# A recurrent attention and expert block: new places for the first batch's transposes, the output weights' maximum, two stores, and VectorE's normalisation

## The reference

```python
xn = (x - mean(x)) / sqrt(var(x) + 1e-5)
q, k, v = split(xn @ Wqkv.T + b_qkv)
scores = q k^T / sqrt(32) + alibi_bias, masked to the lower triangle
s = (softmax(scores) @ v) @ Wout.T + b_out
e = argmax(softmax(xn @ w_router.T))            # one expert for each token
h = xn @ w_fc[e].T ;  a = where(h >= 0, h, h/2) ** 2
g = silu(top_weight * (a @ w_proj[e].T))
out = x + s * g
```

## Time and profile before

| | |
|---|---|
| median of 3 runs | 1421.49 us (1421.0 to 1421.74) |
| profiled execution | 1422.13 us, its span 1420.4 us |
| busy: PE, DVE, ACT, POOL | 1364.2 us (96%), 932.4 (66%), 777.3 (55%), 684.0 (48%) |
| attention passes 1 to 6 | 82.65 us each |
| PE waits named in the whole span, the largest | 14.6 us at the first rows, 8.8 us scores on masks, 3.8 us psT L547 on DVE am L892, 3.4 us psA L437 on DVE xn L869 |

### The profile page before, as it was taken

One profiled execution on the slowest core, in us unless ns is written; L12 is line 12 of the kernel. 1 busy time (PEld: TensorE's weight loads), 2 busy tenths in 40 slices (PEclk: granted clock), 3 DMA queues, 4 the chain that ended last, 5 costly groups with the idle time before them and its releaser, 6 DMA issues.

```text
span 1420.4 us, 30128 instructions
## 1 busy us (share of the span) xinstructions
PE 1364.2 (96%) x9775; PEld 872.8 (61%) x9775; DVE 932.4 (66%) x2456; ACT 777.3 (55%) x1835; POOL 684.0 (48%) x894
## 2 busy tenths in 40 slices
PE   4879999999999999999799999999999999999997
PEld 3446556655655665565466666666666666666665
DVE  6768777777777777777778755555445555544444
ACT  4678878787887878787756422323323223232222
POOL 1455666566566656656633444443334433334333
PEclk9989999999999999999999999999999999999999
DMA  4525334343533434354266322221121121112110
GB/s 179 166 60 173 111 120 147 107 142 98 179 105 120 149 105 142 98 149 130 99 225 212 109 58 55 57 61 33 43 57 54 51 59 53 39 44 56 49 34 30
DMA packets 119458, 140.56 MB, mean 99 GB/s; under 512 B 48655, under 2 KB 97807, under 8 KB 117136
## 3 DMA queue, kind: packets, MB, share of 16 engines
q1 hardware_dynamic: 110368, 112.81, 26.5%
q0 software_dynamic: 8944, 25.83, 5.9%
HBM read 97.81 MB, written 33.95 MB: 93 GB/s over the span
## 4 chain that ended last, share of the span: by engine, by line
PE 82%; DVE 7%; POOL 4%; ACT 3%; issue 2%; DMA 1%; SPq 0%; DVEq 0%; POOLq 0%
PE psF L1280 23%; PE psY L1300 23%; PE psA L373 20%; PE psT L474 7%; PE psA L489 5%; PE psS L453 3%; POOL pr L1082 2%; DVE pr L990 1%; PE psA L437 1%; POOL pre L1099 1%; DMA pt<-in_wqkv 1%; DVE xT L876 1%; ACT xT L597 1%; ACT cf L588 1%; POOL rstd L1091 1%
## 5 line engine op out<-in xcount | busy, mean ns | idle before, releaser
L1280 PE MATMUL psF<-xT,wf 128*128 128x256 f16 (+1 forms) x3264 | 368.0, 269 | 0.0
L1300 PE MATMUL psY<-wf,aT 128*128 x1584 | 363.9, 379 | 0.4 <-DVE aT L1460 0.4
L1280 PEld LDWEIGHTS psF<-xT,wf 128*128 x3264 | 311.9, 98 | 63.6
L1534 POOL TENSOR_TENSOR a<-a 128x512 f32<-128x512 f32 (+1 forms) x136 | 156.0, 1147 | 371.9 <-DVE a L1451 371.4
L1082 POOL TENSOR_SCALAR pr<-pr,rden 128x128 f32<-128x128 f32 (+3 forms) x512 | 263.8, 532 | 137.8 <-DVE rden L1001 136.5
L639 ACT ACTIVATE pr<-pr,mn 128x128 f32<-128x128 f32 (+3 forms) x512 | 282.1, 554 | 0.0
L1300 PEld LDWEIGHTS psY<-wf,aT 128*128 128x128 f16 x1584 | 154.5, 98 | 158.9 <-issue 1.1
L990 DVE CUSTOM_DVE_ANT_0 pr<-psS,base,nsl 128x128 f32<-128x128 f32 (+3 forms) x512 | 249.9, 543 | 1.4 <-PE psS L453 0.6
L474 PE MATMUL psT<-conf,pr 128*128 128x128 f32 x1280 | 204.3, 278 | 5.9 <-POOL pr L1082 3.2
L1365 ACT ACTIVATE rl<-psF 128x512 f32<-128x512 f32 (+1 forms) x136 | 79.3, 583 | 223.3 <-PE psF L1280 216.2
L474 PEld LDWEIGHTS psT<-conf,pr 128*128 128x128 f32 x1280 | 158.0, 142 | 67.4 <-POOL pr L1082 13.4
(11 more groups left out here) (178 smaller groups left out, 1304.6 us busy)
## 6 DMA issues: line engine op xcount, KB each, us to landing
qk_parts<-pre SPq DMA_DIRECT2D x64, 256.0 KB, 2.7
qs<-qk_parts SPq DMA_DIRECT2D x128, 128.0 KB, 2.7
ks<-qk_parts SPq DMA_DIRECT2D x128, 128.0 KB, 2.7
wst<-in_wf SPq DMA_DIRECT2D x16, 1024.0 KB, 5.2
wstage<-in_wf SPq DMA_DIRECT2D x32, 512.0 KB, 4.8
xin<-in_x SPq DMA_DIRECT2D x32, 256.0 KB, 4.1
attn_out<-so SPq DMA_DIRECT2D x32, 256.0 KB, 2.1
xT<-wstage SPq DMA_TRANSPOSE x216, 2.3
```

The lines of the kernel that those rows point to most:

```text
L1280: last = nc.tensor.matmul(psF[c % 2][:, k * TT:k * TT + tn], w(e, 2 * hc, hl, kc * 512 + col, P), xT[:, r % 2, x, kc, 0:tn], start=(m == 0 ...
L1300: last = nc.tensor.matmul(psY[r % 2][h][:], aT[:, c % 4, x, k, h * P:(h + 1) * P], w(e, 2 * hc + 1, hl, q * 512, 512), start=(c == 0 and k ...
L1534: nc.gpsimd.tensor_tensor(at, at, at, ALU.mult).then_inc(s["a_ready"], 1)
```

## The change

- `stack`: the waits and the store become a function `store(w)`. For the first two head groups of batch 0 (u < 2) both stores are issued before the first read; for all others the order stays q store, q reads, k store, k reads.
- `late` goes: the `x` jobs of pass 0 are issued where they are in other passes, before the scores and with `ptrans(b, g, j, 1)` inside them.
- The maximum of the output weights moves from step 9 to step 11, `turn_maxima` from step 10 to 13, `spread_maxima` from step 12 to 14, the instructions that read them from 11 and 13 to 13 and 14. `low_parts(6, 7)` stays at step 11, now behind the maximum instead of behind the first reading; `low_parts(7, 8)` stays at step 14.
- `ln_apply` moves, in passes 0 to 6, from behind `turned(2)` to ahead of the step's read-outs.

```diff
+            def store(w):
+                wait(sp, s["qk_hi"], u * 2 + 1 + w)
+                wait(sp, s["qk_lo"], u * 2 + 1 + w)
+                wait(sp, stacked[w][par], (b * 2 + g // 2) * 64)
                 sp.dma_start(io["qk"][w, par].rearrange("a p n -> p a n"),
                              pre[:, w, :, :]).then_inc(stored[w], 16)
+            if u < 2:
+                store(0)
+                store(1)
+            for w, dst, parts in ((0, qs, (0, 1, 0, 1)), (1, ks, (0, 0, 1, 1))):
+                if u >= 2:
+                    store(w)
                 wait(sp, stored[w], (u + 1) * 16, s["apart_sp"])
...
-                late = [p for p in todo if b == 0 and JOBS[p][0] == "x"]
-                todo = [p for p in todo if p not in late]
...
-                if b == -1 and step == 10:
+                if b == -1 and step == 13:
                     turn_maxima(slice(2, 3), 2)
-                if b == -1 and step == 12:
+                if b == -1 and step == 14:
                     spread_maxima(1, 2)
...
-                for p in late:
-                    job(b, odd, p, lambda: None)
...
             if step == 11:
+                dve.wait_ge(s["w_in"], 16)
+                nc.vector.tensor_reduce(am[:, 2:3], wo_f[:].rearrange("p g n -> p (g n)"), AX.X, ALU.max,
+                                        apply_absolute_value=True).then_inc(s["absmax"], 1)
+                low_parts(6, 7)
+            if step == 13:
                 dve.wait_ge(s["am_turned"], 2)
                 nc.vector.tensor_reduce(amd[0:1, 0:1], psT[2][0:1, 0:P], AX.X, ALU.max).then_inc(s["am_row"], 1)
-                low_parts(6, 7)
-            if step == 13:
+            if step == 14:
+                low_parts(7, 8)
                 dve.wait_ge(s["am_spread"], 2)
                 setup(ts(amr[:, 2:3], psT[2][:, 0:1], 1e-9, None, ALU.max))
-            if step == 14:
-                low_parts(7, 8)
...
                     if b == -1:
-                        dve.wait_ge(s["w_in"], 16)
                         prepare_late(9)
-                        nc.vector.tensor_reduce(am[:, 2:3], ...).then_inc(s["absmax"], 1)
...
+                if more and b >= 0 and 3 <= step < 7:
+                    ln_apply(step - 3)
                 for args in jobs(b, odd, step, ("q", "k", "x", "o", "logits", "rank")):
                     read_out(*args)
                 turned(2)
...
-                if more and b >= 0 and 3 <= step < 7:
-                    ln_apply(step - 3)
```

More of the change, by code:

```diff
@@ L889, in read_out @@
                     if b == -1:
-                        dve.wait_ge(s["w_in"], 16)
                         prepare_late(9)
-                        nc.vector.tensor_reduce(am[:, 2:3], wo_f[:].rearrange("p g n -> p (g n)"), AX.X, ALU.max,
-                                                apply_absolute_value=True).then_inc(s["absmax"], 1)
                 elif kind == "rank":
```

## The result

The changed kernel took 1412.2 us (median of 4 runs, 1411.68 to 1416.01) where the old one took 1421.24: a ratio of 0.9947, interval 0.9935 to 0.9960. A second set of the same kernel gave 1411.16 against 1420.65: 0.9935 (0.9921 to 0.9949). The forecast was 1410.0, in a range from 1406.5 to 1415.5; 11.5 us were to be won and 9.0 to 9.5 were.

What follows compares the result with a forecast made beforehand. TensorE holds 82% of the chain, so gains come only where it waits. 1422.13 - 4.6 - 0 - 7.0 - 0 = 1410.5 us profiled, 1409.9 for the median, stated as 1410.0; range 1406.5 to 1415.5.

Steps and rivals of the forecast that it cites:

- clock stays low in pass 0: Rival: TensorE's clock stays low in pass 0, so steps 4 to 7 give 2.5 to 5 us; 1413 us, chance 0.27.
- Pass -1, -4.6: Term: with the output weights' maximum later in pass -1, V's third product starts 4.6 us earlier; range -3.0 to -5.2.
- the 53.5 that was named as a sign of being wrong: Sign: a first turn of pass 0 later than 53.5 us would show the forecast wrong; it was expected near 51.7.
- its input was ready near 33.2: Step in pass -1: k's store has its input near 33.2 us, so it is issued at about 33.25 instead of 35.75.
- Both stores first, priced at 0, cover for 1.2: Term: both stores ahead of the reads cost 0 (0 to -0.3); without it head 1's scores come about 1.2 us later.
- Pass 0, -7.0: Term: in pass 0, steps 3 to 7, moved ln_apply and x jobs win 7.0 us; range -2.5 to -7.5.
- Passes 1 to 6, 0.0: Term: moving ln_apply in passes 1 to 6 sums to 0.0 per pass; ends -3.4 and +1.8 us over six passes.
- The two waits that were named: Passes 1 to 6: normalisation held at step 3, about 0.16 us lost; o3's bank wait leaves 0.18 won of 0.56.
- The wait of L437: Passes 1 to 6, step 6: TensorE's 0.56 us wait for the normalised rows, which was to go.
- No new waits: Rival: the new waits do not come in passes 1 to 6, winning 3.4 us more; 1406.6 us, chance 0.11.
- Slower: Rival: ln_apply delays read-outs in every pass, TensorE stands at steps 3 to 6, 12 us lost; 1422.5 us, chance 0.03.
- the same ring: Pass 0, steps 4 to 7: engines wait for each other through x jobs, scores, masks, low parts; VectorE waits 9.6 us.

Runs made afterwards that it cites:

- stores_old: Changed kernel with the old order of stores and reads (q store, q reads, k store, k reads) for the first two head groups; 1414.82 us, ratio 0.9957.
- ln_mix: Changed kernel with ln_apply ahead of the read-outs in pass 0 and at step 5, at its old place in steps 3, 4, 6 of passes 1 to 6; 1407.76 us.
- port_lost: Changed kernel with GpSimd's low part of k in pass -1 made to wait for VectorE's 128x2048 low part; 1414.28 us, ratio 0.9950.
- stores_old_warm: Changed kernel with the old order of stores and reads, plus 18 transposes of a constant on TensorE before the first scores; 1412.64 us, ratio 0.9948.
- ln_old: Changed kernel with ln_apply back at its old place, behind turned(2), in all passes; 1413.38 us, ratio 0.9959.
- again: Changed kernel with no edit, run for more times and the second profile; 1411.16 us, ratio 0.9935.

## Why the prediction was right, and where its steps were off

- *Sum.* -11.6 forecast; -9.0 and -9.5 measured by medians, -11.8 between the old profile and the second new one. Of that last, 1.4 lie ahead of the changed part: VectorE's low part starts at 31.97 in one and 30.59 in the other, and the starts of all profiles (the first x turns between 12.4 and 14.6 us) vary by 2 us. What is left is -4.4 in a, -6.6 in b, +0.9 in c and -0.2 in the tail, together about -10.4. The two terms that made the sum were thus right within 0.2 and 0.4 us. For the rest of the miss there are three things that the prediction had not priced: the gaps in c, and executions in which the port is lost or the tail runs at half clock. How much of each there is in the medians is not known. The median of the first set, 1412.2, lies outside the band around the forecast (1409 to 1411.5) and nearer to the 1413 of "clock stays low in pass 0", whose mechanism did not come; 1411.16 lies inside it.
- *Pass -1, -4.6.* Measured -4.4 (a, 24.3 to 19.9) where GpSimd has the port. From the start of a, the walk through VectorE's list put the maximum at 7.5, head 0's masks at 10.9, the third V product at 13.2 and the first turn at 19.7 us; in the second profile they are at 7.54, 10.93, 13.18 and 19.86. (The walk begins at 36.36; the row has the maximum at 36.44, 0.08 later, without effect.) Where the port is lost it is -1.3, and the first turn at 54.40 is later than the 53.5 that was named as a sign of being wrong. The step that failed there is "its input was ready near 33.2": the row was right for that execution, but it was the outcome of a race.
- *Both stores first, priced at 0, cover for 1.2.* Mis-sized: it covers 3.3 us in a and 3.1 to 3.7 in the time. The late reads themselves are about 1.6, near the 1.2. The rest, about 1.7, is the clock, which fell in `stores_old` after TensorE had stood 2.79 us for the reads; the prediction had no term for it.
- *Pass 0, -7.0.* Measured -6.6 to q of the next batch. `pv` at 2.36, the x turns ahead, one stretch at half clock in step 7, priced at 0.5 and worth 0.2 to 0.6. `pv` was taken at full clock because TensorE would stand for less time ahead of it; it came so in all twelve new profiles, but the runs below show that the length of a stand alone does not decide it. What the prediction had not said is that its two edits overlap (4.6 and 5.5 alone).
- *Passes 1 to 6, 0.0.* Measured +0.05 us a pass. The two waits that were named came at the two places that were named: 0.29 us for the held normalisation where the cast at 187.83 had suggested 0.16, and 0.22 at o3 where the walk left 0.38 (0.56 less the 0.18 won). The two misses cancel, so that the sum came out at 0 is in part luck. The wait of L437 went. Undoing three quarters of the edit there won the 0.55 that it was for.
- *Rivals.* "Clock stays low in pass 0" did not come at `pv`. "No new waits" is what ln_mix made true (493.7 in c against 497.3: 3.6 us, where the rival said 3.4). None named the race in pass -1, nor the tail at half clock (2 us in one of two profiles). "Slower" needed TensorE to wait for read-outs at four steps; it did so at one.

## What to carry to other kernels

When an instruction is moved earlier on a helper engine, list for each of its places what it now stands before and what it now runs beside: here one of four places won 0.56 us a pass and the three others together gave about as much back, and keeping only the first was worth 3 us. Two edits that open the same ring are not to be added up. Where the old trace has two instructions of VectorE and GpSimd starting within a few hundredths of a microsecond, take both outcomes into the range and look at what is queued behind the loser: the "both stores first" order makes q's reads wait for the loser as well.

## What the runs showed of the hardware that was not expected

- In a near tie the start stamps do not tell who is served: in the second profile VectorE's two-input instruction starts at 30.59, GpSimd's at 30.61, and VectorE is the one held (3.33 instead of 2.34 us). Over eleven profiles with a distance of 0.03 us or less GpSimd was held once. The Trainium skill, "SBUF — State Buffer", section "Who interferes with whom", says that a VectorE instruction with two SBUF inputs contends with a GpSimd instruction that reads SBUF, and that one is blocked for the whole of the other; the trace agrees for either of the two (3.33 is 2.34 and about 1.0 of GpSimd's 1.16, or 1.16 and 2.2 of VectorE's 2.34). It also says that whichever issues first gets the shared pair of ports; at a distance of 0.02 us the start stamps of the traces do not show that order.
- A stand of 2.66 to 3.02 us on TensorE was followed by a V product at half clock in two kernels (4.11, 4.05) and by one at full clock in a third (2.75, port_lost): the same stand costs 1.3 us or nothing. Shorter ones were followed by half clock too: q's and k's 24 matmuls took 6.90 and 6.98 us behind waits of 1.13 and 0.96 us (stores_old_warm, ln_old) and 5.34 behind waits of 1.28 and 1.09 (port_lost, again). The length of the wait alone does not decide it.
- The stretch from batch 7's logits to the expert part, which no edit touches, took 116.5 to 118.5 us in thirteen profiles. In the longest, 5 us of it ran at a granted clock of 0.50. So part of what one execution differs from another by lies there.
